# Two tiles share seven block products in half of product one, and one transposition moves from TensorE to the DMA queue

## The chip, the cores and the metric

The kernel runs on one core of a Trainium2 chip. The metric is the time of one execution on the device in microseconds (us). All engines of the core run their own list of instructions in order and wait for each other by semaphores.

## What is computed

The input x is 2 x 1024 x 2048, the context ctx is 2 x 2048 x 2048, both float32. Cut to what matters:

```
q1 = fake_quant(layernorm(x));  q2 = fake_quant(ctx)        # 8 bits each
x  = x + tanh(g_xattn) * (q1 @ q2)                          # product one
w  = (U * S) @ V.T                                          # 2048 x 2048, rank 512
x  = x + tanh(g_ffn) * (layernorm(x) @ w.T)                 # V (rank 512), then U
```

## The kernel before, in words

The 2048 rows of x are 16 tiles of 128 rows, tiles 0 to 7 for the first batch and 8 to 15 for the second. A tile passes through these steps, each a function named in the code: `load_x` (four DMAs of 128x512 into one of four places of `ring`), `sums1`, `variance1`, `quantise`, `op2` (layer norm and quantising into `qn`, f16), `q_transpose` (a DMA transposition of `qn` into `qT`), `s1` (product one: four units `(t, n)` of 16 matmuls, each unit 512 columns in one PSUM bank), `x1_unit` (VectorE adds the unit to the residual and takes its statistics), `stats2`, `x_hi` and `x_lo` (second layer norm, split into two f16 halves in `xs`), `x_transpose`, `mm3` (48 matmuls with V), `hid_hi` and `hid_lo` (its result split into `hs`), `h_transpose`, `mm4` (four units of 12 matmuls with U), `y_unit` (VectorE, into `ring`) and `store`. Ahead of `x1_unit` GpSimd adds corrections to the residual (`pre_row`, `pre`).

Each engine's order is written out by hand at the end of its block. TensorE's order around the change is: mm3(3), s1(4), mm4(2), s1(5), mm4(3), mm3(4), units (6,0) and (6,1), mm3(5), the other six units of tiles 6 and 7, mm4(4), `h_pieces(5)`, mm3(6), mm4(5). All DMA transpositions, stores and loads of x share SyncE's queue, in order. Beside this, ScalarE streams the second batch's context: `refill` issues a load of 512 KB, `stream` converts chunks from the places `stage` into `u8r` (eight places).

For tiles 10 to 15 the kernel already takes product one two tiles at a time: for each half of the columns a `quad` of seven block products (P1 to P7, of 8 matmuls each) with sums T1 to T4 of context blocks and S1 to S4 of row blocks, made by VectorE, stands in for eight block products. In those products `add_product` adds each product to the residual.

For tile 5, h is transposed on TensorE: `h_pieces(5)` makes eight 128x128 transpositions into a PSUM bank and `hT_copy(5)` on ScalarE moves them to SBUF.

Of the kernel before, what the change touches and what calls it, by code (L numbers as in the profile page):

```python
# [7 lines left out]
def gated_block_program(nc, x, ctx_in, params, U_t, S, V, out):  # L8
# [18 lines left out]
    R = 4  # L27
    G = 3
    NST = 10
    H_PE = (5,)  # L30
# [15 lines left out]
    with es:  # L46
# [79 lines left out]
        hT_written = sem("hT_written")  # L126
        hT_copied = sem("hT_copied")
# [22 lines left out]
        p_done = sem("p_done")  # L150
        p_read = sem("p_read")
# [38 lines left out]
        unit = lambda t, n: G * n + t if t < G else 6 * NQ + MIXED.index((t, n)) if t in (6, 7) else NQ * t + n  # L190
        part_count = lambda t, h=1: 2 * t + h + 1 if t < G else 2 * G + t - G + 1
# [6 lines left out]
        unit_bank = lambda t, n: bank[4 * (n % 2) + t] if t < G else bank[(unit(t, n) - NQ * G) % 3]  # L198
# [4 lines left out]
        h_dma = lambda u: u + 1 - sum(v <= u for v in H_PE)  # L203
# [11 lines left out]
        S1_END = lambda t: unit(t, NQ - 1) + 1  # L215
# [6 lines left out]
        Q_ACT = range(TB, NT)  # L222
# [14 lines left out]
        t4_room = xs[:, :, :, :].rearrange("p g a w -> p (g a w)")  # L237
        t_part = lambda room: room.rearrange("p (k w) -> p k w", k=KH)
# [26 lines left out]
        def _(pool):  # L265
            def op2(c):
# [10 lines left out]
                if b > 0:  # L277
                    pool.wait_ge(s1_done, unit(TB * b - 1, n) + 1)
# [48 lines left out]
        def _(sp):  # L327
# [30 lines left out]
            def x_transpose_half(u, g):  # L358
# [20 lines left out]
            def h_transpose(u):  # L379
# [8 lines left out]
                elif u in h_home:  # L388
                    sp.wait_ge(s1_done, S1_END(u))
# [166 lines left out]
        def _(pe):  # L556
# [39 lines left out]
            def s1_part(t, n, k0=0, k1=KT):  # L596
                i = unit(t, n)
                if k0 == 0:
# [5 lines left out]
                    else:  # L604
# [60 lines left out]

            def quad(q):
# [3 lines left out]
            def mm3(u):  # L670
# [8 lines left out]
                if u - 2 in H_PE:  # L679
                    pe.wait_ge(hT_copied, H_PE.index(u - 2) + 1)  # L680
# [33 lines left out]
            def h_pieces(u):  # L714
                if u == H_PE[0]:
                    pe.wait_ge(ident_ready, 1)
                pe.wait_ge(h_hi, u + 1)
                pe.wait_ge(h_lo, u + 1)
                dst = h_bank(u)[:, :].bitcast(f16)
                for k in range(2 * RT):  # L720
                    mm = nc.tensor.transpose(dst[:, k * P:(k + 1) * P], hs[:, k, :], ident[:, :])
                mm.then_inc(hT_written, 1)

            def mm4(u, n0=0, n1=NQ):
                if u in H_PE:
                    pe.wait_ge(hT_copied, H_PE.index(u) + 1)
                else:
                    pe.wait_ge(hT_in, 16 * h_dma(u))
# [85 lines left out]
            s1(4)  # L814
            mm4(2)
            s1(5)
# [7 lines left out]
            h_pieces(5)  # L824
# [30 lines left out]
        def _(act):  # L855
# [37 lines left out]
            def quantise(t):  # L893
                act.wait_ge(ln1_ready, t - Q_ACT[0] + 1)
                act.wait_ge(qT_in, 16 * (t - G))
                if t == TB:
# [52 lines left out]

            def hT_copy(u):  # L950
# [788 lines left out]
```

## Time and profile before

| | |
|---|---|
| three runs of the kernel | 587.01, 588.17 and 588.31 us, median 588.17 |
| the profiled execution | 587.26 us, its span of instructions 585.4 us |
| TensorE busy | 568.0 us, 97% of the span |
| granted TensorE clock | 1.00 of full speed (2.4 GHz) |
| VectorE, ScalarE, GpSimd busy | 76%, 40%, 33% of the span |

Busy time says how long an engine worked, not whether others waited for it. TensorE is nearly never idle, so what counts is the number of its matmuls and whether it is made to wait at a place where it did not before.

### The profile page before, as it was taken

The page shows a single profiled execution, that of the slowest core. Times are in us where ns is not written, and L with a number is a line of the kernel's source. Part 1 is how long each engine was busy: PE and PEld are TensorE (multiplying, and loading weights), DVE is VectorE, ACT ScalarE, POOL GpSimd, SP SyncE. Part 2 cuts the span into 40 slices and gives each one's busy share as a digit, 9 for nine tenths or more (in the row PEclk, how much of TensorE's full clock was granted, in tenths as well). Part 3 has the DMA queues.
Part 4 walks back from the last instruction along what each step waited for, and adds up shares of the span by engine and source line. Part 5 has one row for each costly group of instructions (what it writes and reads, how often), then busy time and mean ns, then how long its engine had stood idle before and what let it go on. Part 6 is the DMA issues. An engine that isn't in the chain of part 4 may idle for free.

```text
span 585.4 us, 7495 instructions
## 1 busy us (share of the span) xinstructions
PE 568.0 (97%) x2688; PEld 259.2 (44%) x2688; DVE 445.0 (76%) x796; ACT 236.3 (40%) x269; POOL 194.6 (33%) x146
## 2 busy tenths in 40 slices
PE   1899999999999999999999999999999999999998
PEld 0344444444444444444444444444444444444444
DVE  6878889996178973779978799788597986888222
ACT  4899978822122413648723612102530135003200
POOL 2999750000305127847541720210044005310000
PEclk9999999999999999999999999999999999999999
DMA  8999995638927797789965262423854087403722
GB/s 274 387 387 386 342 275 125 125 112 173 273 73 199 182 239 189 219 231 382 277 158 154 60 138 54 125 73 69 220 108 143 2 179 163 125 1 70 165 55 108
DMA packets 145940, 102.73 MB, mean 175 GB/s; under 512 B 108784, under 2 KB 109040, under 8 KB 145904
## 3 DMA queue, kind: packets, MB, share of 16 engines
q1 hardware_dynamic: 136912, 84.96, 54.9%
q10 hardware_dynamic: 8992, 17.30, 9.0%
q8 instruction: 21, 0.34, 0.2%
q14 instruction: 15, 0.12, 0.1%
HBM read 58.99 MB, written 16.78 MB: 129 GB/s over the span
## 4 chain that ended last, share of the span: by engine, by line
PE 93%; DVE 3%; ACT 1%; POOL 1%; DMA 1%; issue 1%; ACTq 0%; DVEq 0%
PE bank L616 23%; PE bank L692 19%; PE bank L661 11%; PE bank L697 9%; PE bank L755 9%; PE bank L760 9%; PE bank L756 9%; PE bank L579 2%; DMA ring<-in_x_dram 1%; DVE qn L1234 1%; DVE ring L1333 1%; POOL q L279 1%; ACT qn L884 1%; DVE st L1203 0%; PE bank L711 0%
## 5 line engine op out<-in xcount | busy, mean ns | idle before, releaser
L285 POOL TENSOR_SCALAR ring<-ring,bvec 128x2048 f32<-128x2048 f32 x16 | 33.5, 2094 | 260.3 <-DVE bvec L1246 260.3
L616 PE MATMUL bank<-q,qT 128*128 128x512 f16 x512 | 117.6, 381 | 0.0
L692 PE MATMUL bank<-v_hl,xT 128*128 128x512 f16 x448 | 101.3, 379 | 0.0
L290 POOL TENSOR_TENSOR ring<-ring,corr 128x512 f32<-128x512 f32 x64 | 87.1, 1392 | 23.1 <-ACT corr L966 22.1
L755 PE MATMUL bank<-u_hl,hbuf 128*128 128x512 f16 x208 | 78.9, 379 | 0.0
L756 PE MATMUL bank<-u_hl,hbuf 128*128 128x512 f16 x208 | 78.8, 379 | 0.0
L279 POOL TENSOR_SCALAR q<-u8r,const 128x1024 f16<-128x1024 uint8 x52 | 67.2, 1304 | 32.2 <-ACT u8r L863 29.6
L616 PEld LDWEIGHTS bank<-q,qT 128*128 128x128 f16 x512 | 50.3, 98 | 61.1 <-issue 0.8
L692 PEld LDWEIGHTS bank<-v_hl,xT 128*128 128x128 f16 x448 | 43.8, 98 | 52.1
L914 ACT ACTIVATE ln<-ln,const 128x1 f32<-128x1 f32 x16 | 4.7, 293 | 143.6 <-DVE ln L1343 143.6
L1417 DVE SCALAR_TENSOR_TENSOR ring<-bank,cy,ring 128x512 f32<-128x512 f32 x63 | 46.2, 744 | 16.9 <-PE bank L760 16.9
L1373 DVE TENSOR_TENSOR xs<-xn,xs 128x1024 f16<-128x1024 f32 x32 | 47.0, 1468 | 11.0 <-ACT xn L933 6.8
L760 PE MATMUL bank<-u_hl,hbuf 128*128 128x512 f16 x208 | 53.4, 379 | 0.0
L697 PE MATMUL bank<-v_hl,xT 128*128 128x512 f16 x224 | 52.9, 379 | 0.0
L1264 DVE SCALAR_TENSOR_TENSOR ring<-bank,const,ring 128x512 f32<-128x512 f32 x40 | 29.7, 742 | 25.9 <-PE bank L616 22.9
L1203 DVE BATCH_NORM_STATS2 st<-ring 128x6 f32<-128x512 f32 x64 | 40.4, 680 | 7.2 <-DMA ring<-in_x_dram 7.1
L930 ACT ACTIVATE xs<-ring,ln 128x1024 f16<-128x1024 f32 x32 | 38.7, 1234 | 15.5 <-DVE ln L1355 11.5
L1333 DVE SCALAR_TENSOR_TENSOR ring<-bank,const,ring 128x512 f32<-128x512 f32 x42 | 31.3, 745 | 10.8 <-PE bank L661 10.3
L1389 DVE SCALAR_TENSOR_TENSOR hbuf<-bank,hbuf 128x512 f16<-128x512 f32 x16 | 11.0, 687 | 30.2 <-ACT hbuf L947 30.2
L697 PEld LDWEIGHTS bank<-v_hl,xT 128*128 128x128 f16 x224 | 21.9, 98 | 26.4
L579 PE MATMUL bank<-q,ones_h 128*128 128x512 f16 x64 | 19.9, 394 | 12.6 <-POOL q L279 12.5
L863 ACT ACTIVATE u8r<-stage,par,const 128x1024 uint8<-128x1024 f32 x22 | 27.2, 1236 | 11.7 <-ACT u8r L863 4.4
(174 smaller groups left out, 780.5 us busy)
## 6 DMA issues: line engine op xcount, KB each, us to landing
out_dram<-ring SPq DMA_DIRECT2D x63, 256.0 KB, 3.4
ring<-in_x_dram SPq DMA_DIRECT2D x62, 256.0 KB, 4.3
v_hl<-in_ctx_dram SPq DMA_DIRECT2D x26, 512.0 KB, 11.5
stage<-in_ctx_dram ACTq DMA_DIRECT2D x17, 512.0 KB, 5.9
u_hl<-in_L_ffn_V_dram SPq DMA_DIRECT2D x8, 512.0 KB, 11.5
corr<-in_ctx_dram ACTq DMA_DIRECT2D x8, 512.0 KB, 6.4
stage<-in_ctx_dram SPq DMA_DIRECT2D x6, 512.0 KB, 11.4
q<-in_ctx_dram ACTq DMA_DIRECT2D x4, 512.0 KB, 10.1
```

Source lines behind the costliest of these rows:

```text
L279: nc.gpsimd.tensor_scalar(q2_chunk(c), u8r[:, c % NU8, :], C_NC2, 1.0, ALU.add, ALU.mult)\
L290: nc.gpsimd.tensor_tensor(xq(t, n), xq(t, n), corr[:, n * W:(n + 1) * W], ALU.add).then_inc(x1_pre, 1)
L616: mm = nc.tensor.matmul(unit_bank(t, n)[:, :], qT_of(t)[:, k, :], q2[:, n, k, :], start=(k == 0), stop=(k == KT - 1))
L661: mm = nc.tensor.matmul(pbank(q, k)[:, :], left[:, i, :], right[:, i, :], start=(i == 0 and k in (P1, P2, P5)), stop=(i == KH - 1), skip_g ...
L692: nc.tensor.matmul(h_bank(u)[:, :], x_home(u, g)[:, half, k % 8, :], v_hl[:, k, 0, :], start=(g == 0 and a == 0 and half == 0), stop=False)
L697: mm = nc.tensor.matmul(h_bank(u)[:, :], x_home(u, g)[:, 0, k % 8, :], v_hl[:, k, 1, :], start=False, stop=(g == 1 and a == 7))
L755: nc.tensor.matmul(y_bank(i)[:, :], t_hi[:, r, :], u_hl[:, n, r, 0, :], start=(r == 0), stop=False)
L756: nc.tensor.matmul(y_bank(i)[:, :], t_lo[:, r, :], u_hl[:, n, r, 0, :], start=False, stop=False)
L760: mm = nc.tensor.matmul(y_bank(i)[:, :], t_hi[:, r, :], u_hl[:, n, r, 1, :], start=False, stop=(r == RT - 1))
L1203: ins = nc.vector.bn_stats(st1[:, n, :], xq(t, n))
L1373: tt(xs[:, g, 1, :], xn[:, :], xs[:, g, 0, :], ALU.subtract).then_inc(xs_lo, 1)
L1417: stt(xq(u, n), y_bank(i)[:, :], cy[:, n:n + 1], xq(u, n), ALU.mult, ALU.add).then_inc(y_ready, 1)
```

## The change

For tiles 4 and 5 (`EARLY`) the columns 1024 to 2047 (units n = 2 and 3 of both) are computed by seven block products, `early_quad`, which runs after mm4(2) and ahead of units (5,0) and (5,1). Before, these were four units of 16 matmuls. The sums T3, T2, T1, T4 and S1 to S4 are made by VectorE from the first batch's context and from qT, in places that are free then: T3 in `u8r`, T2 in `stage`, T1 in `xs`, T4 in `xT`, the S in `xn` and `qn`. Since `stage` and `u8r` are taken, ScalarE's stream of the second context starts only after P6 and P7 have been read. The quantising pass of tiles 4 to 7 moves from VectorE to ScalarE. `q_transpose(5)` and the loads of tile 5 stand further ahead in SyncE's queue. h of tile 5 is transposed by a DMA after x_transpose(6); `h_pieces` and `hT_copy` are gone.

```diff
-    H_PE = (5,)
+        EARLY = (TB // 2, TB // 2 + 1)
-        Q_ACT = range(TB, NT)
+        Q_ACT = range(R, NT)
...
             def q_transpose(t):
+                elif t - 2 in EARLY:
+                    sp.wait_ge(e_done, NP)
...
             x_transpose(3)
+            store(1, 0)
+            store(1, 1)
+            h_transpose(2)
+            store(1, 2)
+            store(1, 3)
             q_transpose(4)
-            turn(1)
+            for n in range(NQ):
+                load_x(5, n)
             q_transpose(5)
-            turn(2)
+            turn(2, False)
+            h_transpose(3)
             x_transpose(4)
+            q_transpose(6)
             for n in range(NQ):
                 store(3, n)
-            q_transpose(6)
...
+            def early_product(k):
+                a, b = EARLY
+                left, right = {P1: (a_part(a, 0), b_part(2, 0)), P5: (s_part(0), t_part(e_t1)),
+                               P6: (s_part(1), t_part(e_t2)), P3: (s_part(2), b_part(3, 1)),
+                               P7: (s_part(3), t_part(e_t3)), P2: (a_part(a, 1), b_part(2, 1)),
+                               P4: (a_part(b, 1), t_part(e_t4))}[k]
+                if k == P1:
+                    pe.wait_ge(x1_ready, s_unit(a, 1) + 1)
+                elif k == P6:
+                    pe.wait_ge(qT_in, 16 * (b - G + 1))
+                    pe.wait_ge(e_s_made, 2)
+                    pe.wait_ge(e_t2_made, 2)
+                    pe.wait_ge(e_read, e_seq[P1])
...
-            s1(4)
+            s1_part(4, 0)
+            s1_part(4, 1)
             mm4(2)
-            s1(5)
+            early_quad()
+            s1_part(5, 0)
+            s1_part(5, 1)
             mm4(3)
             mm3(4)
...
             mm4(4)
-            h_pieces(5)
             mm3(6)
...
             root1(4)
+            quantise(4)
             op2(4)
-            act.wait_ge(split_lo, VP + RT * NQ)
+            hid_hi(3)
+            root1(5)
+            quantise(5)
+            op2(5)
+            act.wait_ge(e_t4_made, 2)
+            act.wait_ge(e_done, P6 + 1)
             refill(CB)
             refill(CB + 1)
+            act.wait_ge(e_done, P7 + 1)
             stream(0, 2)
-            root1(5)
-            op2(5)
             root2(4)
             x_hi(4)
...
+            def early_t2():
+                for c in range(2):
+                    dve.wait_ge(e_t3_made, c + 1)
+                    tt(k_piece(e_t2, c, 2 * HW), k_piece(e_t3, c, 2 * HW), k_piece(flat2(b_part(2, 0)), c, 2 * HW),
+                       ALU.add).then_inc(e_t2_made, 1)
```

TensorE from the last unit of mm4(2) on. Before (L616 is product one, L760 the last matmuls of a unit of mm4):

```order
219 L760 MATMUL bank<-u_hl,hbuf 128x512 x4
220 L616 MATMUL bank<-q,qT 128x512 x64
```

and now (L718 is `early_product`, L643 product one):

```order
219 L806 MATMUL bank<-u_hl,hbuf 128x512 x4
220 L718 MATMUL bank<-q,qT 128x512 x16
221 L718 MATMUL bank<-stage,qn 128x512 x8
222 L718 MATMUL bank<-xs,xn 128x512 x8
223 L718 MATMUL bank<-u8r,qn 128x512 x8
224 L718 MATMUL bank<-q,xn 128x512 x8
225 L718 MATMUL bank<-xT,qT 128x512 x8
226 L643 MATMUL bank<-q,qT 128x512 x32
```

The row of 64 matmuls was tile 5; the 56 block matmuls and 32 of tile 5 stand there now, and the 64 of tile 4 ahead of mm4(2) have become 32.

VectorE from the statistics of tile 5 (four BN_STATS of L1203) on. Before:

```order
187 L1203 BN_STATS st<-ring 128x6 x4
188 L1210 BN_AGGR ln<-st 128x2
189 L1212 TENSOR_SCALAR ln<-ln 128x1
190 L1213 TENSOR_SCALAR ln<-ln 128x1
191 L1264 SCALAR_TENSOR_TENSOR ring<-bank,const,ring 128x512
192 L1266 BN_STATS st<-ring 128x6
```

and now, from two places ahead of them (L1326, L1334 and L1340 make T2, T1 and T4, L1491 is `hid_lo(3)`, L1310 `x1_unit`):

```order
186 L1326 TENSOR_TENSOR stage<-u8r,q 128x2048 x2
187 L1334 TENSOR_TENSOR xs<-q 128x2048 x2
188 L1491 SCALAR_TENSOR_TENSOR hbuf<-bank,hbuf 128x512
189 L1251 BN_STATS st<-ring 128x6 x4
190 L1258 BN_AGGR ln<-st 128x2
```

`hid_lo(3)`, which waits for mm3(3), has come to stand ahead of tile 5's statistics, behind the sums T2 and T1.

VectorE behind the block products, now (L1369 adds a product, L1445 starts `stats2(4)`, L1472 and L1475 are `x_lo_half(4, 0)`, L1251 the statistics of tile 6):

```order
217 L1372 BN_STATS st<-ring 128x6
218 L1445 BN_AGGR ln<-st 128x2
...
226 L1369 SCALAR_TENSOR_TENSOR ring<-bank,const,ring 128x512
...
228 L1472 TENSOR_SCALAR xn<-ring,ln 128x1024
229 L1475 TENSOR_TENSOR xs<-xn,xs 128x1024
230 L1310 SCALAR_TENSOR_TENSOR ring<-bank,const,ring 128x512
...
232 L1251 BN_STATS st<-ring 128x6 x4
...
236 L1310 SCALAR_TENSOR_TENSOR ring<-bank,const,ring 128x512
...
243 L1519 SCALAR_TENSOR_TENSOR ring<-bank,cy,ring 128x512
```

The last row is `y_unit(3, 0)`: it stands behind the statistics of tiles 4 and 6 and both first units of tile 5.

## Rows read from the trace of the kernel before

**Rows 1.** The page: busy time, and the chain that ended last by engine

```profile
PE 568.0 (97%) x2688; PEld 259.2 (44%) x2688; DVE 445.0 (76%) x796; ACT 236.3 (40%) x269; POOL 194.6 (33%) x146
...
PE 93%; DVE 3%; ACT 1%; POOL 1%; DMA 1%; issue 1%; ACTq 0%; DVEq 0%
```

**Rows 2.** Timeline of TensorE: start, length, line, operation, count

```profile
152.31 13.98 PE L616 MATMUL bank<-q,qT 128*128 128x512 f16 x64
166.13 0.38 PE L755 MATMUL bank<-u_hl,hbuf 128*128 128x512 f16 x1
...
176.49 13.98 PE L616 MATMUL bank<-q,qT 128*128 128x512 f16 x64
...
200.66 3.62 PE L692 MATMUL bank<-v_hl,xT 128*128 128x512 f16 x16
...
217.93 3.62 PE L692 MATMUL bank<-v_hl,xT 128*128 128x512 f16 x16
...
228.29 20.88 PE L616 MATMUL bank<-q,qT 128*128 128x512 f16 x96
...
259.37 0.61 PE L721 MATMUL bank<-ident,hbuf 128*128 128x128 f16 x8
259.81 3.62 PE L692 MATMUL bank<-v_hl,xT 128*128 128x512 f16 x16
```

**Rows 3.** Timeline of TensorE where tiles 10 and 11 take block products

```profile
373.83 3.62 PE L661 MATMUL bank<-q,qT 128*128 128x512 f16 x16
377.45 1.89 PE L661 MATMUL bank<-stage,qn 128*128 128x512 f16 x8
```

**Rows 4.** Waits from 120 to 320 us: who, for what, total, times, longest

```profile
PEld bank L616 <- DMA qT<-qn: 0.3, 1, 0.3
```

**Rows 5.** Landing of DMA transpositions: all into qT from 100 to 330 us, and tile 7's

```profile
DMA to landing us min/median/max: 4.3/5.1/7.5
...
DMA to landing us min/median/max: 6.9/6.9/6.9
```

**Rows 6.** Timeline of SyncE's queue: the issue of tile 7's qn

```profile
221.32 1.91 SPq L356 DMA_TRANSPOSE qT<-qn  x1
```

**Rows 7.** Timeline of VectorE

```profile
128.66 0.81 DVE L1370 TENSOR_SCALAR xn<-ring,ln 128x1024 f32<-128x1024 f32 x1
129.50 1.22 DVE L1373 TENSOR_TENSOR xs<-xn,xs 128x1024 f16<-128x1024 f32 x1
...
139.29 0.26 DVE L1210 BATCH_NORM_AGGREGATE ln<-st 128x2 f32<-128x24 f32 x1
...
141.11 1.35 DVE L1237 TENSOR_SCALAR qn<-ring,ln 128x2048 uint8<-128x2048 f32 x1
...
156.04 0.75 DVE L1264 SCALAR_TENSOR_TENSOR ring<-bank,const,ring 128x512 f32<-128x512 f32 x1 [10.55 <-PE bank L616]
...
192.52 2.46 DVE L1203 BATCH_NORM_STATS2 st<-ring 128x6 f32<-128x512 f32 x4
```

**Rows 8.** VectorE by line and form: count, busy, mean ns, idle before

```profile
L1279 DVE TENSOR_TENSOR q<-q 128x2048 f16<-128x2048 f16 x4 | 4.7, 1218 | 0.0
...
L1318 DVE TENSOR_TENSOR qn<-xn,qT 128x1024 f16<-128x1024 f16 x3 | 2.1, 692 | 0.1
```

**Rows 9.** VectorE's L1401 from 265 to 285 us: shortest, median, longest ns

```profile
L1401 DVE TENSOR_TENSOR xn<-xn,q x6: 676/1338/1422, 266.8 to 274.5; 128x1024 f16<-128x1024 f16 x6
```

**Rows 10.** Timeline of ScalarE: a chunk of context, and tile 8's quantising

```profile
146.54 1.24 ACT L863 ACTIVATE u8r<-stage,par,const 128x1024 uint8<-128x1024 f32 x1 [1.95 <-DMA stage<-in_ctx_dram]
...
286.07 2.09 ACT L900 ACTIVATE qn<-ring,ln 128x2048 uint8<-128x2048 f32 x1 [2.30 <-DVE ln L1223]
288.19 2.00 ACT L890 ACTIVATE qn<-qn,const 128x2048 f16<-128x2048 uint8 x1
```

**Rows 11.** The page's DMA issues: count, KB each, median us to landing

```profile
stage<-in_ctx_dram ACTq DMA_DIRECT2D x17, 512.0 KB, 5.9
...
q<-in_ctx_dram ACTq DMA_DIRECT2D x4, 512.0 KB, 10.1
```

More of the change, by code:

```diff
@@ L493, in _ @@
             x_transpose(6)
+            h_transpose(5)
             for n in range(NQ):
@@ L664, in product, with early_quad @@
                 mm.then_inc(p_done, 1)
+            def early_product(k):
[11 more added lines that the diff above has]
+                    pe.wait_ge(e_read, e_seq[P1])
+                elif k == P5:
+                    pe.wait_ge(e_t1_made, 2)
+                elif k == P7:
+                    pe.wait_ge(e_s_made, 4)
+                    pe.wait_ge(e_t3_made, 2)
+                    pe.wait_ge(e_read, e_seq[P6])
+                elif k == P3:
+                    pe.wait_ge(e_read, e_seq[P5])
+                elif k == P4:
+                    pe.wait_ge(e_t4_made, 2)
+                    pe.wait_ge(e_read, e_seq[P7])
+                for i in range(KH):
+                    mm = nc.tensor.matmul(e_bank(k)[:, :], left[:, i, :], right[:, i, :],
+                                          start=(i == 0 and k in (P1, P2, P5)), stop=(i == KH - 1),
+                                          skip_group_check=k in (P6, P7, P4, P3))
+                mm.then_inc(e_done, 1)
+            def early_quad():
+                for k in range(NP):
+                    early_product(k)
             def quad(q):
@@ L712, in x_pieces @@
                     mm.then_inc(xT_written, 1)
[L714 to L722, printed above, removed]
             def mm4(u, n0=0, n1=NQ):
[L725 to L728, printed above, removed]
+                pe.wait_ge(hT_in, 16 * (u + 1))
                 for n in range(n0, n1):
@@ L1085, in _ @@
             stream(2, 4)
-            hid_hi(3)
+            root1(6)
+            quantise(6)
+            op2(6)
             root2(5)
-            root1(6)
-            x_hi_half(5, 0)
-            op2(6)
-            x_hi_half(5, 1)
+            x_hi(5)
+            hid_hi(4)
             stream(4, 6)
-            hid_hi(4)
             root1(7)
+            quantise(7)
             op2(7)
@@ new lines, in early_add @@
+            def early_add(k):
+                a, b = EARLY
+                t, n = {P1: (a, 2), P5: (b, 3), P6: (a, 3), P3: (a, 3), P7: (b, 3), P2: (a, 2), P4: (b, 2)}[k]
+                if k in (P3, P7, P2):
+                    dve.wait_ge(e_read, e_seq[{P3: P6, P7: P5, P2: P1}[k]])
+                else:
+                    dve.wait_ge(x1_pre, unit(t, n) + 1)
+                dve.wait_ge(e_done, k + 1)
+                stt(xq(t, n), e_bank(k)[:, :], C_A, xq(t, n), ALU.mult, ALU.add).then_inc(e_read, 1)
+                if k in (P3, P7, P2, P4):
+                    dve.wait_ge(e_read, e_seq[k])
+                    nc.vector.bn_stats(st2[:, t % R, n, :], xq(t, n)).then_inc(st2_ready, 1)
@@ L1531, in _ @@
             variance1(4)
+            y_unit(1, 1)
             quantise(4)
-            y_unit(1, 1)
             y_unit(1, 2)
+            early_t3()
+            y_unit(1, 3)
             row_correction(4)
-            y_unit(1, 3)
-            x1_unit(4, 0)
+            early_t2()
+            early_t1()
+            hid_lo(3)
             sums1(5)
             variance1(5)
+            quantise(5)
+            x1_unit(4, 0)
             x1_unit(4, 1)
-            quantise(5)
+            early_t4()
             y_unit(2, 0)
-            x1_units(4, (2, 3))
+            row_correction(5)
+            y_unit(2, 1)
+            early_s_sums()
+            y_unit(2, 2)
+            y_unit(2, 3)
+            early_add(P1)
+            early_s_sums_34()
+            early_add(P6)
+            early_add(P2)
+            early_add(P5)
+            early_add(P7)
+            early_add(P3)
             stats2(4)
-            row_correction(5)
+            early_add(P4)
             x_lo_half(4, 0)
-            y_unit(2, 1)
-            x_lo_half(4, 1)
-            y_unit(2, 2)
-            hid_lo(3)
-            y_unit(2, 3)
-            x1_units(5, range(NQ))
-            variance2(5)
+            x1_unit(5, 0)
             sums1(6)
             variance1(6)
-            scale2(5)
+            x1_unit(5, 1)
+            quantise(6)
             y_unit(3, 0)
-            quantise(6)
+            x_lo_half(4, 1)
+            stats2(5)
             y_unit(3, 1)
+            row_correction(6)
+            x_lo_half(5, 0)
             y_unit(3, 2)
             y_unit(3, 3)
-            row_correction(6)
-            x_lo(5)
-            hid_lo(4)
+            x_lo_half(5, 1)
             sums1(7)
@@ L1567, in _ @@
             quantise(7)
+            hid_lo(4)
             x1_units(6, (0, 1))
```

95 lines of the change are left out of this document (68 added, 27 removed).

## The prediction

> **What bounds the kernel now.** I read the page first: TensorE is busy for 568.0 of 585.4 us, and the chain that ended last is TensorE for 93% [rows 1]. Then the waits of the stretch that the change touches: from 120 to 320 us TensorE waits once, 0.3 us, for a transposition of qn (tile 7's), and for nothing else [rows 4]. Then TensorE's timeline there: every piece starts where the one before ends [rows 2]. So the time falls by what TensorE is spared, and rises by each wait that the new order gives it. VectorE idles beside it, 10.55 us in one piece ahead of the first unit of tile 4 [rows 7].
>
> **Matmuls removed.** 64 matmuls of product one run from 152.31 to 166.13, 0.216 us each [rows 2]. Two tiles by two units were 64 of them, seven products of 8 are 56: 8 x 0.216 = 1.73 us less. That a block product goes at the same pace is seen where tiles 10 and 11 take them [rows 3], but for one thing: P6 starts 3.62 us after P1 where 16 x 0.216 = 3.45 would do. P6 writes the bank that P1's add must have read, and the same turn stands in the new seven. I take 0.17 us for it, with 0 and 0.17 as bounds.
>
> **Transpositions removed.** The eight of h_pieces(5) take from 259.37 to 259.81, 0.44 us [rows 2]. In their place comes a DMA issued behind x_transpose(6), once unit (6,3) is done. I cost it at nothing: the transposition of xs of tile 6 must land before mm3(6) anyway, and mm4(5) needs h only behind mm3(6), 10.4 us later, against 4.3 to 7.5 us to landing [rows 5]. The ScalarE copy that goes with it lay beside TensorE.
> The row gives 0.055 us for each of these transpositions in a run. The Trainium skill (TensorE: Matmul & The Clock Gate, Part 4: PE-mode transpose) gives about 275 ns for one in a kernel's context; by that the eight would be 2.2 us and the change would gain 3.9 us in place of 2.2. The trace does not agree, and the row decides.
>
> **The new clock of TensorE, if nothing waits.** From 152.31 on: two units of tile 4 to 159.22, mm4(2) (48 matmuls, 10.36 us, the distance of 166.13 and 176.49 [rows 2]) to 169.58, where P1 starts; P6 starts at 173.03; the seven end at 181.67, two units of tile 5 at 188.58, mm4(3) at 198.94, where mm3(4) starts (200.66 now). Each later piece is 1.73 us earlier than now, and from mm3(6) on 2.17. For each I ask whether what it needs is there.
>
> **Is tile 5's qT there for P6?** This is the new demand: qT of tile 5 was needed at 176.49 and is now, with S1 and S2 made from it, at 173.03. hid_lo(3) waits for the end of mm3(3), 152.31, and with ScalarE's hid_hi ends about 1.5 us later (two passes of some 0.7 us), 153.8. Tile 5's loads, issued right behind q_transpose(4), are no longer behind tile 2's h and should be in by then. The four statistics 2.46 us [rows 7], 156.3; aggregate and scalars 1.8 us (139.29 to 141.11 [rows 7]), 158.1; quantise and op2 on ScalarE 2.09 and 2.00 [rows 10], 162.3; the transposition 4.3 to 7.5 [rows 5], 166.6 to 169.8; S1 and S2 0.69 each when alone [rows 8] and up to 1.42 each beside GpSimd [rows 9], so 168.0 to 172.6. Margin 0.4 to 5.0 us. I take no wait, since the row of the nearest kind (median 5.1) leaves over 3 us.
> The sums T3, T2, T1 (six passes of 1.22 us [rows 8]) fall into the idle 10.55 us and the time ahead of it. Four of them lie beside GpSimd's pre(4): L1401, the same operation at half the width, takes 0.68 us alone and 1.34 in the median beside GpSimd [rows 9], so 2 x 1.22 for each at worst, and the last ends near 154 to 156. At the worst this takes 2 us of the margin.
> The Trainium skill says why (SBUF — State Buffer, Who interferes with whom): a VectorE instruction with two SBUF inputs and a GpSimd instruction that reads SBUF exclude each other for the whole instruction. By that, too, four sums would pay a GpSimd pass each, and the sum stays as it is; it speaks against the change only where the margin is gone.
>
> **VectorE behind the seven.** ScalarE may refill `stage` only when P6 is done, about 174.9. A chunk lands in 5.9 us in the median [rows 11], the first near 179.5 to 180.8; two conversions of 1.24 [rows 10] with their issues of 0.4, 182.8 to 184.1, and only then comes root2(4), on which VectorE's stats2(4) waits. Behind it stand, on VectorE: root and scalars 1.4, the add of P4 with statistics 1.4, x_lo_half(4,0) 0.81 + 1.22 [rows 7], x1_unit(5,0) 1.4, statistics of tile 6 2.46 and 0.6, x1_unit(5,1) 1.4, scalars 1.1, y_unit(3,0) 0.75 [rows 7]: 12.5 us, so y_unit(3,0) ends at 195.3 to 196.6. mm4(3)'s fourth unit needs it, for y has three banks, at 188.58 + 7.77 = 196.35. Cost 0 to 0.3 us; I take 0. Then x_lo_half(4,1), 2.1 us, and its transposition: 197.4 to 198.7 plus 4.3 to 7.5, 201.7 to 206.2. The second half of mm3(4) needs it at 198.94 + 5.18 = 204.12: with the median 5.1 it lands at 202.5 to 203.8. Bounds 0 and 2.1 us, taken 0.
>
> **Tile 5's xs and tile 7's qT** wait now for stores and loads behind mm4(3), and that ends 1.73 us earlier, so they move along. Tile 7's qn is issued at 221.32 and lands 6.9 us later, at 228.2, for a unit wanted at 228.29 less 0.3 [rows 2, 4 to 6]. In the new order two context loads leave the stretch where tile 7's loads land, and ScalarE's pass is 2.09 us where VectorE's was 1.35 [rows 7, 10]. I take 0, bounds 0 and 1.7.
>
> **Sum.** -1.73 - 0.44 + 0.17 = -2.0 us. The profiled execution took 587.26 us, 1.86 outside its span, which I leave as it is: 585.3. The median of the runs shown, 588.17, is 0.9 above the profiled one, so against it the same gain gives 586.2.
>
> **Rivals.**
> *One: the gain is spent at the hand-over of tile 7 (or tile 5's xs).* For it: the only wait of the stretch is there [rows 4], so no slack exists. If tile 7's qT lands when it does now, TensorE stalls 1.73 us and only 0.27 us is left: 587.9, no change. Against it: the transposition's own chain starts at mm4(3), which moves. Decided by the landing, later than 226.6 costs one for one. Chance 0.15, with part of the loss included.
> *Two: slower, by VectorE's pile behind root2(4).* root2(4) stands behind two chunks of context on ScalarE. If these chunks land like those into `q`, 10.1 us [rows 11], the chain shifts by 4.2 us over the median: y_unit(3,0) ends at about 200.8, mm4(3) stalls 4.4 us, and the result is 590.6. It turns the sign from a landing of 7.7 us on (then the stall passes 2.0). For it: DMA queues are busy and y_unit(3,0) has no slack. Against it: chunks took that long only when four or more of them were queued together. Chance 0.12.
> *Three: P6 waits for qT of tile 5.* Transposition at 7.5, S at 1.42 and T sums doubled together give 172.6 + 2 = 174.6, a stall of 1.6 us: 587.8. Each has to go badly. Chance 0.06.
> *Four: the matmuls go but TensorE is not spared* (block products at another pace): 588.2. The rows of tiles 10 and 11 exclude nearly all of it [rows 3]. Chance 0.02.
> *Forecast:* no stall over 0.8 us in sum. Chance 0.65, 585.2 to 587.0.
>
> **Numbers.** About 0.2% (1.2 us) is what a measurement of this kernel tells from no change. The forecast counts as faster, and a third of rivals one and three (part losses): 0.70. Within 0.2%: 0.17, the rest of one, three and four and a mild form of two. Slower by more: 0.13, which is two and what is unforeseen of its kind. The range reaches from 585.1 (all margins hold, P6 without its 0.17 and the spread of the runs) to 588.8, which takes in rivals one and three whole and the mild part of two.
>
> **What would show it.** In the changed kernel's trace, the seven products in 12.1 to 12.3 us; no wait of TensorE on DVE or DMA between 152 and 230 us beyond the 0.3; no L721; mm3(6) starting 2 us earlier. Wrong would be shown by a gap ahead of P6 (tile 5's qT or the S sums late), a gap inside mm4(3) whose releaser is y_unit's add, one ahead of the second half of mm3(4) or ahead of unit (7,0).

## The result and the profile after

The changed kernel took 593.64 us in the median of five runs against 587.05 us (586.86 to 588.31) for the kernel before on the same chip. Four of its runs lie between 592.8 and 593.8; the fifth, a slow one of 602.67 us, is left out of the ratio. That ratio is 1.0096, with a 95% interval of 1.0083 to 1.011. The change makes the kernel slower by 1%, outside the predicted range of 585.1 to 588.8.

The page of the changed kernel, profiled at 592.8 us:

```profile
span 591.0 us, 7491 instructions
...
PE 568.7 (96%) x2672; PEld 258.7 (44%) x2672; DVE 455.4 (77%) x807; ACT 243.7 (41%) x272; POOL 196.0 (33%) x146
...
PE 82%; DVE 8%; DMA 4%; ACT 3%; issue 2%; POOL 1%; ACTq 0%; SPq 0%; DVEq 0%
```

TensorE runs 16 instructions fewer, but is busy for no less time, and the chain now goes through VectorE, DMA and ScalarE for 15%, where it was 5% [rows 1]. Its timeline in the changed kernel:

```profile
50.97 0.60 PE L602 MATMUL bank<-q,ones_h 128*128 128x512 f16 x2 [1.05 <-DVE q L1304]
...
153.13 7.07 PE L643 MATMUL bank<-q,qT 128*128 128x512 f16 x32
...
170.40 3.62 PE L718 MATMUL bank<-q,qT 128*128 128x512 f16 x16
173.85 1.89 PE L718 MATMUL bank<-stage,qn 128*128 128x512 f16 x8
...
182.48 7.07 PE L643 MATMUL bank<-q,qT 128*128 128x512 f16 x32
...
198.71 0.39 PE L801 MATMUL bank<-u_hl,hbuf 128*128 128x512 f16 x1 [1.39 <-DVE ring L1519]
...
222.28 5.30 PE L751 MATMUL bank<-v_hl,xT 128*128 128x512 f16 x16 [3.53 <-DMA xT<-xs]
...
265.40 3.62 PE L751 MATMUL bank<-v_hl,xT 128*128 128x512 f16 x16
```

L643 is a unit of product one, L718 an early block product, L801 and L806 mm4, L751 mm3. mm3(6) starts at 265.40 where it started at 259.81 [rows 2]: 5.59 us late, and no more is lost behind it, since the whole span is 5.6 us longer (591.0 against 585.4). The 5.59 add up as follows (distances of starts, less 0.22 for a matmul in between):

- +0.82: unit (4,0) starts at 153.13, not 152.31. The row at 50.97 holds a stall on a conversion of context by VectorE, which the change does not touch; such a stall stood in 6 of the 18 profiled executions of these kernels (1.1 to 1.3 us).
- -1.73: the seven products take 12.08 us (170.40 to 182.48), exactly 56 x 0.216.
- +1.55: inside mm4(3), TensorE waits for y_unit(3, 0) (L1519).
- +3.70: ahead of mm3(5), it waits for the DMA of the first half of tile 5's xs.
- +1.68: behind that wait it runs at half the granted clock (1.2 GHz in place of 2.4): the 16 matmuls take 5.30 us where they took 3.62.
- -0.44: the transpositions of h_pieces(5) are gone.

The sum is 5.58. The half clock shows in the table by windows of the changed kernel (each row: window, its length, busy time of TensorE, its weight loads, VectorE, ScalarE and GpSimd, then the granted clock, the DMA share and GB/s):

```profile
216.00:220.00 4.00, 2.74 (x13) 1.07 (x11) 3.65 (x12) 1.54 (x2) 0.00 (x0) 1.00 1.14 230
220.00:224.00 4.00, 1.72 (x5) 0.73 (x6) 2.25 (x4) 3.97 (x4) 0.61 (x1) 0.80 1.17 305
224.00:228.00 4.00, 4.00 (x16) 1.58 (x14) 0.00 (x0) 1.34 (x2) 3.92 (x4) 0.77 1.50 97
```

Waits of the changed kernel from 120 to 320 us, where the kernel before had one of TensorE [rows 4]:

```profile
ACT u8r L911 <- DMA stage<-in_ctx_dram: 20.4, 2, 19.9
...
PE bank L751 <- DMA xT<-xs: 3.5, 1, 3.5
...
PE bank L801 <- DVE ring L1519: 1.4, 1, 1.4
DVE xn L1349 <- DMA qT<-qn: 1.4, 1, 1.4
...
PEld bank L643 <- DMA qT<-qn: 0.2, 1, 0.2
```

**Why the xs of tile 5 is late.** SyncE's queue, first in the kernel before, then in the changed one:

```profile
204.95 2.31 SPq L331 DMA_DIRECT2D ring<-in_x_dram  x4
207.37 10.07 SPq L372 DMA_TRANSPOSE xT<-xs  x2
```

```profile
202.28 3.40 SPq L369 DMA_TRANSPOSE qT<-qn  x1
205.73 3.86 SPq L418 DMA_DIRECT2D out_dram<-ring  x4
209.63 2.67 SPq L342 DMA_DIRECT2D ring<-in_x_dram  x4
212.42 9.42 SPq L387 DMA_TRANSPOSE xT<-xs  x2
221.94 1.25 SPq L407 DMA_TRANSPOSE hbuf<-hbuf  x1
223.29 3.06 SPq L369 DMA_TRANSPOSE qT<-qn  x1
```

Its first half leaves at 212.42 in place of 207.37 and lands 9.72 us later. Ahead of it stand tile 7's loads, which wait for tile 3's stores, and these for tile 3's y units on VectorE (L1417 before, L1519 after), first before and then after:

```profile
199.48 2.14 DVE L1417 SCALAR_TENSOR_TENSOR ring<-bank,cy,ring 128x512 f32<-128x512 f32 x3
```

```profile
197.91 0.74 DVE L1519 SCALAR_TENSOR_TENSOR ring<-bank,cy,ring 128x512 f32<-128x512 f32 x1
...
203.42 0.74 DVE L1519 SCALAR_TENSOR_TENSOR ring<-bank,cy,ring 128x512 f32<-128x512 f32 x1
...
204.20 0.81 DVE L1472 TENSOR_SCALAR xn<-ring,ln 128x1024 f32<-128x1024 f32 x1
205.04 2.87 DVE L1475 TENSOR_TENSOR xs<-xn,xs 128x1024 f16<-128x1024 f32 x1
207.84 1.39 DVE L1519 SCALAR_TENSOR_TENSOR ring<-bank,cy,ring 128x512 f32<-128x512 f32 x2
```

Units 1 to 3 were done by 201.6 and are now by 209.2, since the change writes x_lo_half(4, 1), stats2(5), row_correction(6) and x_lo_half(5, 0) between them. SyncE's own waits say the same: it waits 2.1 us for L1519 ahead of two of the four stores, and 1.0 us for the landing of stores ahead of two of the loads. The first two stores are not held by VectorE. They stand behind the transposition of tile 6's qn, which occupies the queue for 3.40 us from 202.28, where the kernel before has the stores ahead of it.

**Why y_unit(3, 0) is late.** ScalarE in the changed kernel:

```profile
175.83 0.95 ACTq L918 DMA_DIRECT2D stage<-in_ctx_dram  x2
183.15 1.24 ACT L911 ACTIVATE u8r<-stage,par,const 128x1024 uint8<-128x1024 f32 x1 [19.95 <-DMA stage<-in_ctx_dram]
...
184.84 1.24 ACT L911 ACTIVATE u8r<-stage,par,const 128x1024 uint8<-128x1024 f32 x1 [0.45 <-DMA stage<-in_ctx_dram]
...
186.53 0.29 ACT L966 ACTIVATE ln<-ln,const 128x1 f32<-128x1 f32 x1 [0.45 <-ACT u8r L911]
```

The two chunks of context land 7.2 and 8.2 us after their issue, and root2(4) (L966), which stands behind their conversions, comes at 186.53. VectorE waits 3.81 us for it, and y_unit(3, 0) ends at 198.65.

### The profile page after: what moved, and what is told of

The parts are those of the page before. It is cut to its first block, busy times and chain, and to the rows that moved or that the text cites. A ratio compares the mean times of both kernels' runs of the same rounds, so it can differ in the third digit from the quotient of the medians.

```text
span 591.0 us, 7491 instructions
## 1 busy us (share of the span) xinstructions
PE 568.7 (96%) x2672; PEld 258.7 (44%) x2672; DVE 455.4 (77%) x807; ACT 243.7 (41%) x272; POOL 196.0 (33%) x146
## 4 chain that ended last, share of the span: by engine, by line
PE 82%; DVE 8%; DMA 4%; ACT 3%; issue 2%; POOL 1%; ACTq 0%; SPq 0%; DVEq 0%
PE bank L751 18%; PE bank L643 15%; PE bank L688 11%; PE bank L756 9%; PE bank L801 9%; PE bank L802 9%; PE bank L806 9%; DMA xT<-xs 2%; DVE st L1251 1%; PE bank L602 1%; DMA stage<-in_ctx_dram 1%; ACT u8r L911 1%; DVE q L1304 1%; PE bank L718 1%; DVE ring L1435 1%
## 5 line engine op out<-in xcount | busy, mean ns | idle before, releaser
L751 PE MATMUL bank<-v_hl,xT 128*128 128x512 f16 x448 | 102.9, 384 | 3.5 <-DMA xT<-xs 3.5
L643 PE MATMUL bank<-q,qT 128*128 128x512 f16 x448 | 104.2, 382 | 0.0
L801 PE MATMUL bank<-u_hl,hbuf 128*128 128x512 f16 x208 | 78.9, 379 | 1.4 <-DVE ring L1519 1.4
L751 PEld LDWEIGHTS bank<-v_hl,xT 128*128 128x128 f16 x448 | 44.2, 99 | 57.4 <-issue 6.3
L643 PEld LDWEIGHTS bank<-q,qT 128*128 128x128 f16 x448 | 44.2, 99 | 53.8 <-issue 1.7
L1519 DVE SCALAR_TENSOR_TENSOR ring<-bank,cy,ring 128x512 f32<-128x512 f32 x63 | 46.2, 744 | 16.9 <-PE bank L806 16.9
L966 ACT ACTIVATE ln<-ln,const 128x1 f32<-128x1 f32 x16 | 4.7, 292 | 129.8 <-DVE ln L1445 129.4
L806 PE MATMUL bank<-u_hl,hbuf 128*128 128x512 f16 x208 | 53.4, 379 | 0.0
L756 PE MATMUL bank<-v_hl,xT 128*128 128x512 f16 x224 | 52.9, 379 | 0.0
L1475 DVE TENSOR_TENSOR xs<-xn,xs 128x1024 f16<-128x1024 f32 x32 | 43.9, 1373 | 11.1 <-ACT xn L985 6.9
L1251 DVE BATCH_NORM_STATS2 st<-ring 128x6 f32<-128x512 f32 x64 | 40.0, 679 | 3.7 <-DMA ring<-in_x_dram 3.6
L1435 DVE SCALAR_TENSOR_TENSOR ring<-bank,const,ring 128x512 f32<-128x512 f32 x42 | 31.3, 745 | 10.2 <-PE bank L688 10.2
L1310 DVE SCALAR_TENSOR_TENSOR ring<-bank,const,ring 128x512 f32<-128x512 f32 x36 | 26.7, 742 | 12.2 <-PE bank L643 9.7
L1491 DVE SCALAR_TENSOR_TENSOR hbuf<-bank,hbuf 128x512 f16<-128x512 f32 x16 | 11.0, 688 | 32.2 <-ACT hbuf L997 32.1
## 6 DMA issues: line engine op xcount, KB each, us to landing
v_hl<-in_ctx_dram SPq DMA_DIRECT2D x26, 512.0 KB, 11.5
u_hl<-in_L_ffn_V_dram SPq DMA_DIRECT2D x8, 512.0 KB, 11.5
q<-in_ctx_dram ACTq DMA_DIRECT2D x4, 512.0 KB, 10.9
```

Of the source, the lines that this page charges most:

```text
L643: mm = nc.tensor.matmul(unit_bank(t, n)[:, :], qT_of(t)[:, k, :], q2[:, n, k, :], start=(k == 0), stop=(k == KT - 1))
L751: nc.tensor.matmul(h_bank(u)[:, :], x_home(u, g)[:, half, k % 8, :], v_hl[:, k, 0, :], start=(g == 0 and a == 0 and half == 0), stop=False)
L756: mm = nc.tensor.matmul(h_bank(u)[:, :], x_home(u, g)[:, 0, k % 8, :], v_hl[:, k, 1, :], start=False, stop=(g == 1 and a == 7))
L801: nc.tensor.matmul(y_bank(i)[:, :], t_hi[:, r, :], u_hl[:, n, r, 0, :], start=(r == 0), stop=False)
L806: mm = nc.tensor.matmul(y_bank(i)[:, :], t_hi[:, r, :], u_hl[:, n, r, 1, :], start=False, stop=(r == RT - 1))
L1251: ins = nc.vector.bn_stats(st1[:, n, :], xq(t, n))
```

## The experiments

The theory after these rows: the loss is made by the place of tile 3's y units 1 to 3 on VectorE, through stores and loads in SyncE's queue to the hand-over of tile 5's xs. Rivals: the transfer is slow by what runs beside it, wherever it is issued; or the chunks ahead of root2(4) are the cause of all.

**The base.** In these kernels each transposing DMA is replaced by a plain one of the same bytes in blocks of 256 bytes, repeating the first block, so the transposing is left out. In SyncE's queue it is lighter, too: for tile 6's qn it occupies 0.6 us, the transposing one 2.84 us before and 3.40 after the change:

```diff
+            def stand_in(dst, src):
+                blocks = src.rearrange("p (k w) -> p k w", w=P)
+                return sp.dma_start(dst, blocks[:, 0:1, :].to_broadcast([P, dst.shape[1], P]))
...
-                sp.dma_start_transpose(qT_of(t), qn[:, :]).then_inc(qT_in, 16)
+                stand_in(qT_of(t), qn[:, :]).then_inc(qT_in, 16)
```

> The kernel before with each of its DMA transpositions replaced by a plain DMA of the same bytes in blocks of 256 bytes (each destination block gets the first block of the source), so the data are not transposed and the output is not the reference's; everything else, waits included, is unchanged. It is the base for the runs to come. I expect landings of 3.5 to 5 us, no new wait of TensorE, and 585 to 589 us. If the plain copies are much slower than the transpositions it shows as waits of TensorE ahead of mm3 and product one, above 595 us, and the base is of no use.

> The changed kernel with the same stand-in for each DMA transposition (data not transposed). If both gaps (ahead of y_unit(3,0)'s reader near 197 us, and ahead of mm3(5) near 218 us) come from order and traffic, not from the transposing itself, they appear here too: 2 to 7 us over the same base. If they depend on the transposition being slow under load (9.7 us to landing), the second gap is gone here and only 1.5 us of stall against 2.0 us of removed work stays: within 1 us of the base.

The base of before took 587.68 us (ratio 1.0002, 0.9989 to 1.0015) and can serve as a base, though the first half of tile 5's xs landed in 9.2 us and not in the expected 3.5 to 5. The changed one took 588.09 (1.000, 0.9988 to 1.0012). So with easier transfers the loss is gone, and in the medians so is the gain. In its trace the first half of tile 5's xs still leaves 4.5 us later than in its base (210.65 against 206.16) but lands in 6.3 us. TensorE then starts mm3(5) 0.24 us late and the second half of mm3(5) 0.50 us late (the row with 0.3 below), while y_unit(3, 0) costs 0.85 us:

```profile
PE bank L805 <- DVE ring L1523: 0.7, 1, 0.7
PE bank L755 <- DMA xT<-xs: 0.3, 1, 0.3
```

**The same transfer made slower, in both kernels.** The first half of tile 5's xs, and this alone, in blocks of 128 bytes (d0, d1; the diff) and of 64 (d10, d9; 4 in place of the 2):

```diff
-                         flat2(xs[:, g, :, :])).then_inc(xT_in[g], 16)
+                         flat2(xs[:, g, :, :]), 2 if (u, g) == (5, 0) else 1).then_inc(xT_in[g], 16)
```

> The kernel before with stand-ins for its transfers that transpose (plain transfers of the same bytes in blocks of 256 bytes, which leave out the transposing), and the stand-in for the first half of tile 5's xs in blocks of 128 bytes, twice as many, so that it takes longer. In the kernel before with plain stand-ins this transfer was issued at 206.16 and landed at 215.39 against a need at about 218. Theory (the loss is a late hand-over of tile 5's xs that the kernel before has room for): same time as before within 0.3%, 587 to 589 us, any stall ahead of mm3(5) under 1 us. Rival (the slower transfer alone costs, wherever it is issued): 589.5 us or more.

> The changed kernel with the same stand-ins, tile 5's first half in blocks of 128 bytes. With plain stand-ins it landed at 216.91 with an issue at 210.65, and the changed kernel was level with the one before. Theory: it now lands at 220 to 223, TensorE stands 2.5 to 4.5 us ahead of mm3(5), half a clock for up to 2 us follows, and the time is 590 to 594 us, ratio 1.004 to 1.010. Rival (the loss of the change comes from elsewhere, the tile 3 y units or chunks alone): 588 to 589 us as with plain stand-ins.

> The changed kernel with stand-ins, tile 5's first half in blocks of 64 bytes, four times as many as plain. Theory: the time follows the landing of this one transfer: landing 2 us or more behind that of d1_after (220.08), idle time ahead of mm3(5) 5 us or more, and as in the changed kernel itself (3.5 us idle, half a clock for 3.4 us) TensorE then starts at 1.2 GHz, 593 to 597 us. Rival (the blocks' size does not set the landing, the company does): within 0.7 us of d1_after's 590.59 us.

> The kernel before with stand-ins and tile 5's first half in blocks of 64 bytes, the transfer that cost the changed kernel 5.06 us of idle time and the half clock (593.29 us). Theory: issued at about 207 it lands at 217.5 to 219.5 against a need at 217.9, idle time 0 to 1.7 us, 587.5 to 589.5 us, so at least 4 us below the changed kernel with the same transfer. Rival (so slow a transfer costs the kernel before as much): 592 us or more.

| tile 5's first half | before: issue, landing | before, us | changed: issue, landing | changed, us |
|---|---|---|---|---|
| 256 bytes | 206.16, 215.39 | 587.68 | 210.65, 216.91 | 588.09 |
| 128 bytes | 207.11, 216.31 | 587.59 | 210.84, 220.08 | 590.59 (1.0031 to 1.0071) |
| 64 bytes | 206.22, 217.73 | 587.45 (0.9992 to 1.0011) | 211.59, 222.66 | 593.29 (1.0088 to 1.0115) |

The slowest takes about as long in either kernel, 11.5 and 11.1 us. The kernel before starts mm3(5) at 217.87, 0.12 us late; the changed one issues the transfer 5.4 us later and pays 5.06 us and the half clock. All four expectations held. At 128 bytes the transfer is no slower than at 256 in the kernel before (9.2 us both), but 3 us slower in the changed one; why is not shown. The waits and one window of the changed kernel at 64 bytes:

```profile
PE bank L757 <- DMA xT<-xs: 4.9, 1, 4.9
PE bank L807 <- DVE ring L1525: 1.5, 1, 1.5
```

```profile
222.00:228.00 6.00, 5.20 (x13) 1.88 (x14) 0.21 (x1) 2.39 (x3) 5.48 (x4) 0.50 0.96 225
```

So the transfer's length alone costs nothing up to 11.5 us; with the change's issue time it reproduces the result of 1%.

**Two single repairs of the transfer, on d1.** d2 issues it ahead of tile 7's loads, d3 takes the two chunks of stream(4, 6) ahead of hid_hi(4):

```diff
+            x_transpose_half(5, 0)
             for n in range(NQ):
                 load_x(7, n)
-            x_transpose_half(5, 0)
             x_transpose_half(5, 1)
```

> As the changed kernel with the slow first half, and that transfer issued ahead of the four loads of tile 7's x in SyncE's queue. Theory: issued at about 208 instead of 211 to 212, it gives back 2 to 4.5 us of the loss, 587 to 590 us, and the stall ahead of mm3(5) is under 1.5 us. Rival (it is the amount of transfer beside it, not the order of issue): no more than 1 us given back.

> As the changed kernel with the slow first half, and the two ctx chunks stream(4, 6) taken ahead of hid_hi(4) on ScalarE again, so that their refills (two transfers of ctx) leave before tile 5's xs does. Theory of the late issue: the first half still leaves at 211 or later; the shorter company gives back 0 to 1.5 us. Rival (the refills beside the transfer set its landing): 2 to 4 us given back, 587 to 590 us.

d2: 590.26 us (1.0031 to 1.0071), nothing gained though the first half lands in time at 213.60; tile 7's loads get late, and TensorE waits for the second half and for tile 7's q:

```profile
PE bank L649 <- DMA qT<-qn: 2.1, 1, 2.1
PE bank L757 <- DMA xT<-xs: 1.1, 1, 1.1
```

My number for it (587 to 590, a stall under 1.5 us) was wrong: the late thing is the whole queue, not one transfer in it. d3: 589.88 us (1.002 to 1.0052); the first half leaves at 216.03 (1.7 us of this is a later start of this execution, unit (4,0) at 154.07 against 152.34 in d1) and lands in 5.65, with 2.5 us of wait. The landing is shorter, and the later issue takes it back. The 0.7 us given back lie in the range of the late issue (0 to 1.5), not in that of the rival (2 to 4).

**The y units moved, on d1 and on the plain base.**

```diff
             x_lo_half(4, 1)
-            stats2(5)
             y_unit(3, 1)
-            row_correction(6)
-            x_lo_half(5, 0)
+            stats2(5)
             y_unit(3, 2)
             y_unit(3, 3)
+            row_correction(6)
+            x_lo_half(5, 0)
             x_lo_half(5, 1)
```

> On the changed kernel with stand-ins and the slow first half (590.59 us, first half of tile 5's xs issued at 210.84, TensorE idle 3.07 us ahead of mm3(5)): tile 3's y units 1, 2 and 3 on VectorE ahead of stats2(5), row_correction(6) and the low half of tile 5's xs, where the changed kernel puts them between and behind these. Theory (the transfer leaves late because tile 7's loads ahead of it in SyncE's queue wait for tile 3's stores, and these for y units that the change moved back by 4 us and more): stores, loads and the first half leave 1.5 to 3 us sooner, the idle time ahead of mm3(5) falls to 1.5 us or less, 588 to 589.5 us. Rival (xs itself, whose low half is now made later, sets the issue, or the transfers beside it set the landing): idle time stays over 2.5 us, 590 us or more.

> The edit of d4_y3 alone (tile 3's y units 1, 2 and 3 ahead of stats2(5), row_correction(6) and tile 5's xs on VectorE) on the changed kernel with plain stand-ins (588.09 us). Theory: 586 to 587.3 us, ratio to before 0.996 to 0.999, no more than 0.3 us of idle time ahead of mm3(5), the stall of 0.6 to 0.9 us in mm4(3) still there. Rival (with plain stand-ins there was little to win): 587.6 us or more.

d4: 586.62 us, ratio 0.9984 (0.9971 to 0.9997), 4 us less than d1 and more than I had expected (588 to 589.5). s8: 587.0 us, 0.9984 (0.9972 to 0.9996), as expected. So with stand-ins this version is 0.16% faster than the kernel before. Of the 4.3 us by which the first half lands earlier in d4 than in d1 (215.8 against 220.1, unit (4,0) at 152.27 and 152.34), only 1.3 us are an earlier issue; the other 3 are a shorter landing (6.2 against 9.24), which I had not forecast and can't explain. d4's waits of TensorE, and s8's timeline at mm3(6), 1.49 us ahead of 259.56 in s0h_before:

```profile
PE bank L807 <- DVE ring L1525: 0.8, 1, 0.8
```

```profile
258.07 3.62 PE L755 MATMUL bank<-v_hl,xT 128*128 128x512 f16 x16
```

Terms for s8: -1.73 - 0.44 + 0.93 for the stall left in mm4(3) = -1.24, and 0.25 us by which unit (4,0) starts sooner in this execution (151.81 against 152.06).

**The y units alone, in the kernel before.** The converse, on d0:

```diff
             y_unit(3, 1)
-            y_unit(3, 2)
-            y_unit(3, 3)
             row_correction(6)
-            x_lo(5)
+            x_lo_half(5, 0)
+            y_unit(3, 2)
+            y_unit(3, 3)
+            x_lo_half(5, 1)
```

> The kernel before with stand-ins and the slow first half (587.59 us, first half issued at 207.11, landed 216.31), and tile 3's y units 2 and 3 on VectorE behind row_correction(6) and the low first half of tile 5's xs, as the change places them. Theory (the place of these y units alone makes the late hand-over): the stores and tile 7's loads leave 3 to 5 us later, the first half at 210 to 211 and lands at 218.5 to 221, TensorE idles 1 to 3.5 us ahead of mm3(5), 588.5 to 591 us. Rival (it takes the change's other shifts too): idle time under 0.5 us, 587.3 to 588 us.

592.49 us, ratio 1.0082 (1.006 to 1.0103): the place of two short instructions makes a loss about as large as the whole change's. The sign was as expected; the size (588.5 to 591) and the place were not. Here q of tile 6 stands behind tile 3's stores, and it is what lands late, ahead of unit (6,0). The half clock follows there too: the 32 matmuls take 8.71 us where 7.07 would do.

```profile
207.00 0.99 SPq L409 DMA_DIRECT2D out_dram<-ring  x2
208.09 0.60 SPq L331 DMA_DIRECT2D qT<-qn  x1
208.74 6.18 SPq L337 DMA_DIRECT2D ring<-in_x_dram  x4
```

```profile
215.47 8.71 PE L622 MATMUL bank<-q,qT 128*128 128x512 f16 x32 [3.53 <-DMA qT<-qn]
```

The changed kernel has q_transpose(6) ahead of these stores, so it was spared that one. So d8 shows that the place of y units alone can cost this much through SyncE's queue, by another victim than in the changed kernel.

**The limit of the repair.** The y units ahead, with the transfer in blocks of 64 bytes:

> The changed kernel with the same transfer in blocks of 64 bytes, and tile 3's y units 1 to 3 moved ahead as in d4_y3. Theory: the issue about 1.5 to 2 us sooner and less company give back 3 us or more of 593.29: 587.5 to 590 us, idle time ahead of mm3(5) 0.5 to 3 us, no half clock. Rival (with so slow a transfer the place of the y units no longer decides): 592 us or more.

592.25 us (1.0057 to 1.01), only 1 us given back: the expectation failed and the rival's 592 or more came true. The first half now leaves at 209.91, 1.7 us sooner than in d9 but still 3.7 us behind the kernel before, lands 11.3 us later, and TensorE waits 3.95 us, with the half clock. So the place of y units 1 to 3 makes only 1.7 of the 5.4 us by which the changed kernel issues this transfer later. For the rest the traces only suggest a cause: the stores stand behind the second half of x_transpose(4) and behind q_transpose(6), so that the first leaves at 201.79 where it left at 196.97 (d10). No run tests this. The lateness of y_unit(3, 0) is not it: with that unit moved ahead as well (d7, below) the first half leaves 57.2 us behind the start of unit (4,0), and 57.3 us in d4. In the changed kernel itself the landing took 9.7 us and q_transpose(6) occupied the queue for longer than here, so whether the repair would be enough there is not shown. Issue ahead of the loads together with the y units ahead was not tried.

**What delays y_unit(3, 0).** root2(4) and x_hi(4) ahead of stream(0, 2) on ScalarE, and y_unit(3, 0) ahead of x1_unit(5, 1), on d4 and on s8; then without the ScalarE part:

```diff
-            stream(0, 2)
             root2(4)
             x_hi(4)
+            stream(0, 2)
             stream(2, 4)
```

> As d4_y3, and also what delays tile 3's first y unit taken out: root2(4) and x_hi(4) on ScalarE ahead of the two ctx chunks of stream(0, 2) instead of behind them, and y_unit(3, 0) on VectorE ahead of x1_unit(5, 1) and quantise(6). Theory: the stall of 0.59 to 0.97 us ahead of mm4(3)'s second part goes, and with it 0.6 to 1 us; the time is 587 to 588.5 us. Rival (the chunks only get late elsewhere, or q6 does): no more than 0.3 us below d4_y3.

> The three edits of d5_y3_root on the changed kernel with plain stand-ins, which was level with the kernel before at 588.09 us. Theory (the eight block products' worth of TensorE time, 1.73 us, and 0.44 us of transposes are a real gain that the waits eat): 585.8 to 587.2 us, ratio 0.996 to 0.999, no idle time over 0.5 us ahead of mm3(5) or in mm4(3). Rival (other waits take their place): 587.5 us or more.

> As d4_y3 (slow first half, 586.62 us), and y_unit(3, 0) on VectorE ahead of x1_unit(5, 1) and quantise(6), but root2(4) left where the change has it, since ahead of the chunks it made these late. Theory: the stall of 0.93 us in mm4(3) goes and nothing takes its place, 585.6 to 586.5 us. Rival (tile 6's q, or the second part of s1(5)'s readers, get late in its place): 586.8 us or more.

d5 591.56 us (1.0042 to 1.0082) and s7 590.5 (1.0015 to 1.0066): both expectations missed, and both rivals (other waits take its place) held. The stall in mm4(3) does go, but the chunks' refills leave about 4 us later (186.51 in s7 against 182.48 in s8), ScalarE waits for them ahead of tile 6's root1, and the stall comes back ahead of tile 4's and tile 5's xs. d5's ScalarE and TensorE:

```profile
ACT u8r L917 <- DMA stage<-in_ctx_dram: 5.7, 2, 3.0
```

```profile
PE bank L757 <- DMA xT<-xs: 4.6, 2, 3.7
```

d7: 588.16 us (0.9985 to 1.0032), which can't be told from the kernel before and misses the expected 585.6 to 586.5; the 0.93 us stall is gone, and 1.2 us of wait for tile 5's xs stands in its place. Its runs went from 585.54 to 591.89, a wide spread.

**The h of tile 5 by DMA, alone.** On d0:

> The kernel before with stand-ins and the slow first half, and of the change only the part on tile 5's h: moved by a transfer, not as eight pieces on TensorE and a copy on ScalarE. Predicted for it alone: 0.44 us saved, 587.2 us against 587.59 us. Rival (it adds a transfer to a busy stretch, and mm4(5) waits for it, or the q and xs transfers beside it land later): 588 us or more.

586.77 us (ratio 0.9989, 0.9978 to 1.0) against 587.59 for d0 (1.0001, 0.999 to 1.0012), so the intervals overlap. The traces tell more: mm4(4)'s last group is followed at once by mm3(6), where d0 has 0.45 us of transpositions, no wait appears, and from unit (4,0) to mm3(6) pass 107.06 us (152.13 to 259.19), where d0 has 107.50 (153.03 to 260.53). The predicted 0.44 us is what the traces show.

**The clock.** Bursts of 96 equal matmuls on TensorE, parted by waits for ScalarE, in a kernel of its own that computes nothing of the reference:

> A kernel of its own, not the reference's computation: eight bursts of 96 matmuls of 128x512 with gaps of 1, 2, 3, 4, 6, 3 and 2 ScalarE passes of about 1.2 us each between them. It prices an idle stretch of TensorE. Theory: the 3.7 us gap ahead of mm3(5) is what halved the granted clock for the next eight matmuls (0.43 us each in place of 0.216), so gaps of about 4 us and more are followed by matmuls at 0.43 us, for some 3.4 us, and gaps of about 1.2 and 2.4 us by none. Rival (the fall has another cause, the load of the chip): the bursts behind all gaps, or behind none, start at half clock.

```profile
30.33 20.89 PE L69 MATMUL bank<-right,left 128*128 128x512 f16 x96 [1.38 <-ACT junk L58]
53.69 22.58 PE L69 MATMUL bank<-right,left 128*128 128x512 f16 x96 [2.47 <-ACT junk L58]
79.83 20.89 PE L69 MATMUL bank<-right,left 128*128 128x512 f16 x96 [3.56 <-ACT junk L58]
105.37 22.52 PE L69 MATMUL bank<-right,left 128*128 128x512 f16 x96 [4.65 <-ACT junk L58]
134.71 23.20 PE L69 MATMUL bank<-right,left 128*128 128x512 f16 x96 [6.82 <-ACT junk L58]
161.47 20.89 PE L69 MATMUL bank<-right,left 128*128 128x512 f16 x96 [3.56 <-ACT junk L58]
184.84 20.89 PE L69 MATMUL bank<-right,left 128*128 128x512 f16 x96 [2.47 <-ACT junk L58]
```

A burst takes 20.89 us at the full clock. Three of them took 1.6 to 2.3 us more, behind 2.47, 4.65 and 6.82 us of idle time, and the four behind 1.38, 3.56, 3.56 and 2.47 us nothing. The length of an idle time alone doesn't tell if the clock falls. Neither the theory (4 us and more, not 2.4) nor the rival (all or none) holds as written: both gaps of over 4 us were followed by the half clock, but so was one of 2.47 us. This is a single execution.

## Why the prediction was wrong

- **Matmuls removed** (-1.73): right, 12.08 us for seven products. The 0.17 for P6's bank turn did not appear (3.45 us from P1 to P6).
- **Transpositions removed** (-0.44, DMA at no cost): right; the DMA left at 259.38 and landed 3.1 us later, unmissed.
- **P6 and tile 5's qT, rival three** (no wait taken): right. It was issued at 163.22 and landed in 4.3 us, the shortest of the bounds and by that luckier than the 5.1 it was taken at; VectorE waited 1.4 us for it, TensorE never.
- **VectorE behind the seven** (0 to 0.3, taken 0): mis-sized, measured 1.55 (0.65 to 1.7 with stand-ins). The step took 5.9 us for a chunk from a median [rows 11] (its 179.5 for the earliest landing rests on no row); they landed in 7.2 and 8.2, beside tile 3's h, issued within the same microsecond. The mechanism of rival two was right, and small. Its point of 7.7 us for a change of sign needed the loss to come from here alone.
- **"They move along"** (tile 5's xs and tile 7's qT, cost 0, bounds 0 and 1.7): this is the step that failed, 3.70 + 1.68 us. The first half of tile 5's xs left 5.05 us later than before (212.42 against 207.37), where the step had it leave 1.73 us sooner. It took the end of mm4(3) as what releases stores and loads. What releases the last stores is the y units, and these stand in VectorE's order behind 5.7 us of passes for tile 4's and tile 5's xs, and a wait of 1.4 us, that stood behind them or elsewhere before; I had added up that order only as far as y_unit(3, 0). That the late hand-over is the cause is shown by d9 and d10: the same slow transfer costs the kernel before 0.12 us, and the changed one, which issues it 5.4 us later, 5.06 us and the half clock. That the place of the y units matters is shown by d4 and d8, by taking it away and by putting it in alone. It is not all of the late issue: d11 gives back 1.7 of 5.4 us of it, and 1 us of time. The step also left out that the change puts q_transpose(6) ahead of the stores. The two context loads that it saw leave come behind this transfer now (213.63 and 215.32), and putting them back gave no more than 0.7 us (d3).
- **Rival one** named this hand-over, but priced it at what was gained, 1.73 us ("lands when it does now"). It could not become a loss in that form, and no rival had the half clock. Tile 7's qT, its first victim, was in time (0.2 us) although it landed in 10.9 us, since TensorE was late by then.
- By size: the two sound steps give -2.17, the missed ones +1.55, +3.70 and +1.68, and 0.82 of the profiled shift was there before the change begins. That start differs between executions (unit (4,0) from 151.81 in s8 to 154.07 in d3), in variants of both kernels (153.07 in d8), so how much of the 0.82 belongs to the changed kernel's median stays open. The medians lie 6.6 us apart, the profiled executions 5.5; the 1.1 between is not explained.

What stays open as well: the real transposing transfers were not varied, only stand-ins, so that the 9.7 us of this landing (beside tile 7's loads and two chunks) is a reading of one trace. In the kernel before the same transfer took 9.8 us, so it is the issue that changed and not the landing.

## What to carry to other kernels

When a change writes new work into one engine's order, add up that order as far as every instruction that a store, a load or a refill waits for, not only to the one that the busiest engine waits for; a cheap instruction that frees a buffer belongs ahead of long ones that nobody awaits yet. A queue that is issued in order hands its delay to each transfer behind, so moving one transfer forward may only name another victim (d2). And a stall of 3 to 4 us of TensorE must be priced with what may follow it at half the clock, here 1.7 us more; behind 3.1 us nothing followed (d1, s7).

## What the runs showed of the hardware

- Idle time and clock: behind 3.5 us or more in front of mm3(5) or unit (6,0), half the clock for 3.4 to 6.8 us (changed kernel, d5, d8, d9, d11); behind 3.1 us, none (d1, s7); in the kernel of bursts, none behind 3.56 and once behind 2.47.
- Landing is not a fixed price. Tile 5's first half in blocks of 128 bytes took 6.2 us when issued at 209.58 (d4) and 9.24 when issued at 210.84 (d1), with tile 7's loads ahead of it and two chunks behind it in both; the second half followed 1.4 us behind it in d4 and 0.7 in d1.
- Quartering the blocks of a plain transfer from 256 to 64 bytes made its landing 11.5 us in place of 9.2 in the kernel before, beside the same loads (s0h, d10); halving them to 128 bytes left it at 9.2 (d0).
